# Full-fp32 channel mix for the last two query tiles, with re-joined weights, in an attention and channel-mix kernel

## What is computed

```python
x = y_all
x = x + attn(layernorm(x))     # q, k, v of 256 channels, causal softmax, Wo
x = x + ffn(layernorm(x))
# ffn, for a row h and the row h_prev before it:
xr = mu_r * h + (1 - mu_r) * h_prev
xk = mu_k * h + (1 - mu_k) * h_prev
out = sigmoid(xr @ W_r.T) * (square(relu(xk @ W_k.T)) @ W_v.T)
```

## Time and profile before

| | |
|---|---|
| median of 3 executions | 362.97 us (362.35 to 363.37) |
| the profiled execution | 362.65 us, span 360.6 us |
| PE busy | 351.1 us (97%), weight loads 321.4 us (89%) |
| DVE, ACT, POOL busy | 260.4, 239.6, 219.6 us |
| granted TensorE clock | full in every slice |
| share of the chain that ended last | PE 86%, DVE 6%, ACT 4% |

### The profile page before, as it was taken

How to read it: one execution, slowest core, us unless ns; L and a number is a source line. 1 busy time by engine, 2 the same in 40 slices (tenths; PEclk the granted TensorE clock), 3 DMA queues, 4 the chain that set the end, 5 groups by cost and what they waited for, 6 DMA issues and landing times.

```text
span 360.6 us, 6804 instructions
## 1 busy us (share of the span) xinstructions
PE 351.1 (97%) x2457; PEld 321.4 (89%) x2457; DVE 260.4 (72%) x571; ACT 239.6 (66%) x468; POOL 219.6 (61%) x258
## 2 busy tenths in 40 slices
PE   8999999999999999999999999999999999999995
PEld 6788888889999798899998889899999999999985
DVE  4698798689666966867718785777776889663655
ACT  2445636787569647678565678587387767899482
POOL 3012531758777655679564357869166967599961
PEclk9999999999999999999999999999999999999999
DMA  7700000000030003004000000210001000000101
GB/s 209 228 2 1 2 0 3 1 2 1 2 116 2 1 2 116 3 0 118 0 3 0 2 0 3 55 63 2 2 0 60 3 0 0 32 31 0 60 0 58
DMA packets 11905, 10.64 MB, mean 30 GB/s; under 512 B 1889, under 2 KB 11874, under 8 KB 11874
## 3 DMA queue, kind: packets, MB, share of 16 engines
q1 hardware_dynamic: 10512, 10.23, 8.9%
q10 hardware_dynamic: 1362, 0.01, 0.2%
HBM read 6.04 MB, written 4.19 MB: 28 GB/s over the span
## 4 chain that ended last, share of the span: by engine, by line
PE 86%; DVE 6%; ACT 4%; issue 2%; POOL 1%; ACTq 0%; DVEq 0%
PE W L821 18%; PE W L824 17%; PE W L825 17%; PE O L1001 8%; PE O L1003 8%; PE O L1002 8%; PE W L857 3%; DVE xhat L620 2%; PE B L972 1%; ACT mix L495 1%; DVE peak L690 1%; DVE h_row L723 1%; PE B L981 1%; ACT st L440 1%; PE O L1026 1%
## 5 line engine op out<-in xcount | busy, mean ns | idle before, releaser
L373 POOL TENSOR_TENSOR p_lo<-st,p_hi 128x512 fp32r<-128x512 f32 (+1 forms) x71 | 81.0, 1159 | 39.1 <-ACT p_hi L440 38.8
L440 ACT ACTIVATE st<-W 128x512 f32<-128x512 f32 (+1 forms) x79 | 42.4, 538 | 47.9 <-PE W L825 45.2
L690 DVE TENSOR_TENSOR peak<-peak,W 128x512 f32<-128x512 f32 (+3 forms) x70 | 42.3, 604 | 43.5 <-ACT st L440 42.9
L1001 PE MATMUL O<-v_hi,p_hi 128*128 128x258 f32 x241 | 69.5, 288 | 0.1
L1003 PE MATMUL O<-v_hi,p_lo 128*128 128x258 f32 x241 | 68.0, 282 | 0.0
L1002 PE MATMUL O<-v_lo,p_hi 128*128 128x256 f32 x241 | 67.7, 281 | 0.0
L824 PE MATMUL W<-xT_lo,kT_hi 128*128 128x512 f32 (+2 forms) x176 | 62.0, 352 | 0.0
L821 PE MATMUL W<-xT_hi,kT_hi 128*128 128x512 f32 (+2 forms) x176 | 61.4, 349 | 0.0
L825 PE MATMUL W<-xT_hi,kT_lo 128*128 128x512 f32 (+2 forms) x176 | 60.0, 341 | 0.0
L391 POOL TENSOR_TENSOR mix_lo<-mix,mix_hi 128x512 fp32r<-128x512 f32 (+2 forms) x36 | 41.2, 1175 | 14.7 <-ACT mix_hi L440 14.7
L440 ACT ACTIVATE p_hi<-st 128x512 fp32r<-128x512 f32 (+1 forms) x71 | 40.4, 569 | 13.3 <-PE O L1003 11.8
(11 more groups left out here) (152 smaller groups left out, 849.2 us busy)
## 6 DMA issues: line engine op xcount, KB each, us to landing
out_dram<-gate SPq DMA_DIRECT2D x15, 256.0 KB, 2.1
x_in<-in_L_attn_y_all_dram SPq DMA_DIRECT2D x7, 512.0 KB, 4.4
x_in<-in_L_attn_y_all_dram SPq DMA_DIRECT2D x2, 256.0 KB, 5.0
h_row<-in_L_attn_Wk_dram SPq DMA_DIRECT2D x1, 256.0 KB, 3.5
h_row<-in_L_attn_Wq_dram SPq DMA_DIRECT2D x1, 256.0 KB, 4.3
st<-in_L_attn_Wv_dram SPq DMA_DIRECT2D x1, 256.0 KB, 5.4
st<-in_L_attn_Wo_dram SPq DMA_DIRECT2D x1, 256.0 KB, 5.8
mix<-in_L_ffn_W_k_dram SPq DMA_DIRECT2D x1, 256.0 KB, 6.7
```

Of the source, the lines that this page charges most:

```text
L373: g.tensor_tensor(lo[:, r], score_tile(u), hi[:, r].bitcast(f32), ALU.subtract).then_inc(p_split, 1)
L440: a.activation(dst, src, ACT.Copy, **kw).then_inc(done, 1)
L690: v.tensor_tensor(peak[:, J % 2, r], peak[:, J % 2, r], scores, ALU.max).then_inc(maxed, 1)
L1001: mm(o[:, 0:VW], hi[:, r], v_hi[:, j + b, :], start=j + b == 0, stop=False)
```

## The change

The two single parts do without splits in their channel mix. Their three products use full fp32 operands: `mix` itself, the squared `h_row` slots, and three whole weight matrices. These whole matrices are made by POOL, as `ffn_hi` + `ffn_lo`, into two input buffers that hold rows of groups 4 and 5 and are no longer needed: W_k and W_v right behind the second residuals of group 4, W_r behind those of group 5. The transposes of the single parts go to the O banks 0 and 1, and DVE mixes from these banks: one column from `hT`, then 127 from PSUM. The tables change for the slots after 74; before that the order is as it was, but for the two additions on POOL.

```diff
-    PV_AT = [..., 74, 74, 74, 96, 132, 134, 158, 186, 188, 188, 188, 189, 189, 189, 189, 192, 192, 193, 193, 193, 194, 194, 194, 195, 203, 203]
-    MT_AT = [..., (135,)]
-    MB_AT = [..., (171,)]
+    PV_AT = [..., 74, 74, 74, 84, 141, 158, 169, 186, 192, 200, 201, 201, 203, 203, 205, 206, 206, 206, 208, 209, 209, 209, 209, 210, 211, 229]
+    MT_AT = [..., (125,)]
+    MB_AT = [..., (178,)]
...
+        whole_k, whole_v = [x_in[:, (NG - 4) % NX, 2 * i:2 * i + 2, :] for i in range(2)]
+        whole_r = x_in[:, (NG - 3) % NX, 0:2, :]
...
+            def unsplit(J, whole, i):
+                pool.wait_ge(out_ready, unit(J, 1) + 1)
+                g.tensor_tensor(whole, ffn_hi[:, i].bitcast(f32), ffn_lo[:, i].bitcast(f32), ALU.add).then_inc(whole_ready, 1)
...
                     elif stage == "ff" and n not in SINGLE:
                         add_x1(n, i)
+                        if i == 1 and PARTS[n][0] == NG - 4:
+                            unsplit(n, whole_k, 0)
+                            unsplit(n, whole_v, 2)
+                        elif i == 1 and PARTS[n][0] == NG - 3:
+                            unsplit(n, whole_r, 1)
...
             def mix_part(J, j):
                 r = span(J)
+                if J in SINGLE:
+                    if j < KC:
+                        sc.wait_ge(mixed, 2 * KC * J + KC)
+                        scaled(J, KC + j, MU_R, j).then_inc(mu_r_done, 1)
+                    return
...
+                if J in SINGLE:
+                    a.activation(single(J, h), bank_of("kk", J, h)[:, r], ACT.Relu).then_inc(k_relu, 1)
+                    return
...
-                if J in SINGLE:
-                    sc.wait_ge(k_ready, KC * (J + 1))
-                    a.activation(act_hi[:, h, r], act[:, h, r], ACT.Square).then_inc(act_high, 1)
...
+                if J in SINGLE:
+                    bank, c = bank_of("hT", J, h), slice(r.start, r.start + 1)
+                    v.scalar_tensor_tensor(mix[:, j, c], hT[:, h, c], cols[:, om, h:h + 1], mix[:, j, c], ALU.mult, ALU.add)
+                    if j >= KC and J < LAST:
+                        v.tensor_copy(hT[:, h, r.stop:r.stop + 1], bank[:, r.stop - 1:r.stop])
+                    c = slice(r.start + 1, r.stop)
+                    v.scalar_tensor_tensor(mix[:, j, c], bank[:, r.start:r.stop - 1], cols[:, om, h:h + 1], mix[:, j, c],
+                                           ALU.mult, ALU.add).then_inc(mixed, 1)
+                    return
...
+                if J in SINGLE:
+                    pe.wait_ge(whole_ready, 1)
+                    pe.wait_ge(mixed, 2 * KC * J + KC)
+                    for k in range(KC):
+                        last = mm(bank_of("kk", J, h)[:, r], whole_k[:, k, h * P:(h + 1) * P], mix[:, k, r], start=k == 0, stop=k == KC - 1)
...
+                if J in SINGLE:
+                    pe.wait_ge(whole_ready, 3)
+                    pe.wait_ge(mixed, 2 * KC * (J + 1))
+                    for k in range(KC):
+                        last = mm(bank_of("rr", J, i)[:, 0:C], mix[:, KC + k, span(J)], whole_r[:, k, :], start=k == 0, stop=k == KC - 1)
...
+                if J in SINGLE:
+                    pe.wait_ge(whole_ready, 2)
+                    for k in range(KC):
+                        pe.wait_ge(single_squared, KC * SINGLE.index(J) + k + 1)
+                        last = mm(bank_of("ff", J, i)[:, 0:C], single(J, k), whole_v[:, k, :], start=k == 0, stop=k == KC - 1)
```

More of the change, by code:

```diff
@@ L182, in attention_channel_mix_block @@
         USES += [("S", s, 0)] if 0 <= s < NS else []
-        USES += [u for u in STAGES[s] if u[0] in ON_PE]
+        USES += [u for u in STAGES[s] if u[0] in ON_PE and (u[0] != "hT" or u[1] not in SINGLE)]
     y_t = y.rearrange("b (n p) c -> p (b n) c", p=P)
@@ L256, in bank_of @@
         def bank_of(*use):
+            if use[0] == "hT" and use[1] in SINGLE:
+                return o_of(PARTS[use[1]][0], use[2])
             return early[1] if use == ("kT", 0, 1) else bank_w[USES.index(use) % NW]
@@ L395, in act_low @@
                 pool.wait_ge(act_high, KC * J + h + 1)
[L396 to L400 removed]
+                g.tensor_tensor(act_lo[:, h, r], act[:, h, r], act_hi[:, h, r].bitcast(f32), ALU.subtract).then_inc(act_split, 1)
             def add_x1(J, i):
@@ L424, in _ @@
                 for stage, n, i in STAGES.get(s - 1, ()):
-                    if stage == "mix" and n < LAST:
+                    if stage == "mix" and n not in SINGLE:
                         mix_low(n, i)
@@ L429, in _ @@
                         rsqrt1(n)
-                    elif stage == "kk" and n < LAST:
+                    elif stage == "kk" and n not in SINGLE:
                         act_low(n, i)
@@ L482, in exps, with scaled @@
                 high(weights(u)[0][:, cols_of(u)], score_tile(u), p_high)
+            def scaled(J, j, mu, h):
+                r = span(J)
+                return a.activation(mix[:, j, r], bank_of("hT", J, h)[:, r], ACT.Copy, scale=cols[:, mu, h:h + 1])
             def hT_part(J, h):
@@ L492, in hT_part @@
                     sc.wait_ge(ffn_ready, 3)
[L494 to L497 removed]
                 if J in SINGLE:
[L500 to L506 removed]
+                    scaled(J, h, MU_K, h).then_inc(mu_done, 1)
+                else:
+                    a.activation(hT[:, h, r.start + 1:r.stop + 1], bank_of("hT", J, h)[:, r], ACT.Copy)
+                    scaled(J, h, MU_K, h)
+                    scaled(J, KC + h, MU_R, h).then_inc(mu_done, 1)
             def mix_part(J, j):
                 r = span(J)
+                if J in SINGLE:
[3 more added lines that the diff above has]
+                    return
                 sc.wait_ge(mixed, 2 * KC * J + j + 1)
[L511 removed]
+                if j == 0 and J > 0:
                     sc.wait_ge(r_ready, unit(J, 0))
                     sc.wait_ge(ff_ready, unit(J, 0))
[L514 to L515 removed]
                 high(mix_hi[:, j, r], mix[:, j, r], mix_high)
@@ L800, in _ @@
                         mix_part(n, i)
-                        if n == LAST and i > 0:
-                            mix_low(n, i - 1)
-                        if n == LAST and i == 2 * KC - 1:
-                            mix_low(n, i)
                     elif stage == "kk" and n in SINGLE:
                         single_square(n, i)
-                        if n == LAST and i == KC - 1:
-                            for h in range(KC):
-                                act_low(n, h)
                     elif stage == "ff":
@@ L887, in hTr @@
                 G, t0, n = PARTS[J]
-                free("hT", J, h)
+                if J not in SINGLE:
+                    free("hT", J, h)
+                elif J == SINGLE[0]:
+                    pe.wait_ge(o_used, G * TG + KC)
+                else:
+                    pe.wait_ge(mixed, 2 * KC * (J - 1) + KC + h + 1)
                 pe.wait_ge(h_ready, TG * G + t0 + n)
```

90 lines of the change are left out of this document (26 added, 64 removed).

## The result

On one chip, 20 executions of each: **363.46 us** for the changed kernel (362.52 to 365.15) and 362.79 for the kernel before (362.32 to 363.49). The ratio is 1.0027, with a 95% interval of 1.0017 to 1.0037. So the change makes the kernel slower by 0.7 us between the medians; the means, 363.81 and 362.80, are 1.0 apart. The forecast was +1.3 (364.2), with a range of 361.4 to 365.5.

The account below looks back on a forecast made before the run. PE was taken to set the pace, with POOL equally close from 312.1 to 337.0 us and a latency-bound tail. Terms 2.2 - 0.3 - 0.6 = +1.3 us gave 364.2 us on the median, range 361.4 to 365.5.

Parts of the forecast that it names:

- What bounds the kernel: PE sets the pace; POOL runs as close from 312.1 to 337.0 us; in the tail PE waits for ACT and DVE.
- Part 1: Near 273 us, two POOL additions behind group 4's residuals delay lo halves; PE waits 2.2 us, all lost.
- the hand-over: Near 273 us, from the end of POOL's lo half to PE's start; taken as about 0.15 us of PE's slack.
- Part 2: Around the peak, third addition and new order: tile 2's last step 1.6 us later, last value matmul at -0.3 us.
- two paths ending at one place: POOL's longer chain and the late peak spread both delay tile 2's last step; losses overlap, together 1.6 us.
- Rival B: Part 1's stall stays but part 2 costs nothing: -0.2 us, 362.8 us, no change; chance 0.16.
- Part 3: Tail from last value matmul to DVE's end: 11.8 us for 12.42, so -0.6, as latency goes.
- 8 of 256 columns at 0.48: In the tail, eight full fp32 matmuls of 256 columns cost PE 3.84 us.
- 0.55 us of waits in the tail: PE waits only about 0.55 us in the tail, mostly for a W bank whose gate DVE multiplies late.
- Rival C: A longer tail: PE waits twice by 0.7 us more for ACT and DVE; +2.7, 365.7 us; chance with D 0.14.
- D: Full matmuls from x_in cost PE 0.1 us more each, 1.6 for 16, partly hidden: 365.0 us; chance with C 0.14.
- Case A: Only the tail counts; parts 1 and 2 fall away: -1.77 - 0.6, about -2.3, 360.6 us; chance 0.14.

Follow-up runs that it names:

- the last one: Changed kernel with W_k and W_v added behind the next four lo halves, W_r near 292 us, peak spread at slot 160; 360.46 us, ratio 0.9928.

## Why the prediction was right, and where it was off

**What bounds the kernel.** Right: the losses show as gaps of PE, and the two large waits named in the profile are the ones forecast, in kind and place. The third (0.22) is that for tile 2's row, 0.49 before.

**Part 1.** Predicted 2.2, measured 2.07, and 0.85 with one addition, 3.29 with three. The delay of the lo halves was forecast as 2.54 + 0.08 = 2.62 and is 2.5 + 0.13 = 2.63, so both terms were right. The 0.1 is the hand-over: PE starts 1.31 us behind the start of the lo halves here, and 1.32 and 1.34 with three additions and with one. The first lo half alone takes about 1.28, so the hand-over is about 0.03 and not 0.15, and the slack was 1.88 - 1.31 = 0.57 and not 0.45. That nothing makes the wait up was shown by moving it (-2.2) and by adding it to the kernel before (+2.2). The estimate of 1.11 us for an addition from the Trainium skill, GPSIMD Engine Reference, section 3.1, is 0.16 too low for each here, where two take 2.54.

**Part 2.** Predicted: last step of tile 2 +1.6 and its transposes +1.45, PE's loss of 1.5 for the values' lo half overlapping with POOL's chain, and -0.3 in all to the last value matmul. Measured: +1.63 at the last step, +1.37 at the transposes, a wait of 1.53, and -0.50. That the two losses overlap was an argument from two paths ending at one place. It is now shown from both sides: without the third addition the end is where it was, and without the late peak spread too. Rival B had the last step of tile 2 come no later; it came 1.63 later. Better placed additions and an earlier peak get back 358.6 - 357.7 = 0.9 us of it.

**Part 3 was mis-sized.** The step "8 of 256 columns at 0.48 (3.84; 14.04 to 15.00 is two)" took half of a distance of 0.96 as the price, and at the end the same form takes 0.43; what the first distance holds besides the matmuls no run shows. Eight of them are 0.4 us less. The 0.55 us of waits in the tail were too many by some 0.3: the chain shows PE or DVE working nearly without a break from 344.94 on, and in the starts the largest wait is 0.19 (355.59 to 356.64 for two matmuls of 256 columns). So the tail is 1.20 shorter where 0.6 was forecast. The 128-column price of 0.22 was right, and DVE's small operations were near it (to the next start 0.13 for one column and 0.27 for 127, forecast 0.15 and 0.35). Rival C, a longer tail, is refuted by the same rows, and so is D, which had these matmuls dearer.

**What the sum did not contain.** At full clock the measured terms are 2.07 - 0.50 - 1.20 = +0.4; the spans say +0.3. The forecast's +1.3 was thus 0.9 too high, for three small errors of the same sign. The measured +0.67 is nearer because of a term that the prediction did not have: behind the wait the clock falls in nearly half of the executions. The prediction read "the granted clock is 1.00 in both" and let it stand, though it put the first gap of 2 us into a stretch in which PE had never stopped. That the centre is only 0.6 off is thus partly luck. The range does not depend on it: the medians of both kinds of execution (363.26 and 364.75) lie within it.

**The chances.** The case held most likely, slower by over 0.3%, had 0.49; the measured ratio of 1.0027 lies in the next one, within 0.3%, which had 0.34, and its interval (1.0017 to 1.0037) reaches over the bound. Case A with 0.14 was too high: PE busy for 40.00 of 40.00 us excludes that a wait there is made up, and the first wait was predicted from a row with 0.12 us of distance. With the additions put elsewhere 360.46 was measured, for 360.6 in A. A's parts explain it only by half: the last value matmul is 1.7 us earlier than before (344.06 for 345.79), as A has it (1.77), but the tail gives 1.2 us and not 0.6, and the kernel before measured 0.3 more beside that run. With its additions and the peak spread placed elsewhere the change is a gain of 2.6 us; where they stand takes it back.

## What to carry to other kernels

When a change puts work on an engine that is half idle, look at what stands behind it in that engine's queue: here the idle stretch came 5 us later, and three additions of 1.3 us and a late spread of the peak cost 3 us by their places. A stretch in which GpSimd is idle is not free if VectorE is then working from SBUF to SBUF and PE soon needs what VectorE does next: of three such places here one cost nothing, one a wait of 0.5 us and one 2 us. Read both timelines before placing anything there. If a fix of one wait gives nothing, look for a second path that ends at the same place before giving it up, and look at every execution's clock and not just at the profiled one.

## What the hardware showed that was not expected

**The clock behind a wait.** In the four kernels whose first wait is 2.07 to 2.09 us, 22 of 41 executions lose clock (9 of 20, 6 of 11, 3 of 4, 4 of 6), at a price of 1.2 to 1.7 us between the median spans; with 3.29 us it is 4 of 11. With no wait over 1.55 us it is none in 36 (the runs with W_r early, W_k and W_v moved, one addition, all moved, and the last one). A wait of 1.96 us at another place (314.3 to 316.4) did not do it in 9. So the fall came only in kernels with a wait of over 2 us, but the length does not decide alone, and 4 in 11 against 22 in 41 is too little to say that a longer one is milder. What else decides is open. The Trainium skill, TensorE: Matmul & The Clock Gate, Part 1, says that the chip's look at activity runs free of the kernel's start. That executions of one kernel differ (9 of 20 in the change) agrees with it.

**VectorE beside GpSimd.** An operation of DVE that reads and writes only SBUF stretches beside an operation of two tensors on POOL: `TENSOR_SCALAR` of 128x256 from 0.41 to 1.37 us, three `SCALAR_TENSOR_TENSOR` of 128x512 from 2.24 to 4.32, and a copy of two columns from 0.17 to 1.11, the last beside `mix_lo` and not beside an addition. It is thus nothing that the change brings: in the kernel before an `h_row` takes 1.36 us at 295.35, beside lo halves. The subtractions that read PSUM do not stretch: in the kernel before four take 2.47 us at 59.97, with POOL idle but for 0.2 us, and 2.47 at 269.02, with POOL at work, and eight take 4.87 in the earlier trace rows and after the change.

**Full fp32 on TensorE.** A matmul is two records and takes 0.43 us for 256 columns and 0.22 for 128 (0.87 for four records, 0.89 for eight), against 0.12 for one of 256 columns with fp32r operands, of which a split product needs three (0.36).
